# Decoder layer on one core: the work behind the value products done once for two tasks, splits before roots, six leading self pairs

## What is computed

```python
x = _layernorm(x + _L0_attn_ref(x, wq, bq, wk, bk, wv, bv, wo, bo))      # self: softmax(q k^T / sqrt(8)) v, then wo
x = _layernorm(x + _L0_xattn_ref(ctx, x, ctx, Wk, Wq, Wv, Wo))           # cross: 8x8 weights per head, then Wo
x = _layernorm(x + _L0_ffn_ref(x, W1, b1, W2, b2))

def _layernorm(x, eps=1e-05):
    m = mean(x); v = var(x)
    return (x - m) / sqrt(v + eps)

def _qlinear(x, W, b):           # twice in _L0_ffn_ref, with an exact gelu between
    xq, sx, zx = _affine_quantize(x)      # scale from min and max over the whole tensor
    wq, sw = _sym_quantize(W)
    return einsum('bsh,oh->bso', xq - zx, wq) * (sx * sw) + b
```

## Time and profile before

| | us |
|---|---|
| median of 3 runs | 369.61 |
| lowest and highest | 368.77, 369.62 |
| the profiled execution | 368.67 |
| its span, first to last instruction | 366.9 |
| DVE busy | 328.6 (90%) |
| PE busy | 267.3 (73%) |
| ACT busy | 255.5 (70%) |
| POOL busy | 189.1 (52%) |

### The profile page before, as it was taken

One profiled execution on the slowest core, in us unless ns is written; L12 is line 12 of the kernel. 1 busy time (PEld: TensorE's weight loads), 2 busy tenths in 40 slices (PEclk: granted clock), 3 DMA queues, 4 the chain that ended last, 5 costly groups with the idle time before them and its releaser, 6 DMA issues.

```text
span 366.9 us, 13218 instructions
## 1 busy us (share of the span) xinstructions
PE 267.3 (73%) x4899; PEld 170.7 (47%) x4899; DVE 328.6 (90%) x718; ACT 255.5 (70%) x504; POOL 189.1 (52%) x382
## 2 busy tenths in 40 slices
PE   3669878998888988889888898888783466102960
PEld 2446545565655655656565565555452121001540
DVE  5657798899999999999999999999989599998994
ACT  2126877687878878788787888778672499605965
POOL 5244778566665665656666566665222005400385
PEclk9999999899999999999999999999997586755995
DMA  1352332324233233232332324332000000000024
GB/s 50 99 153 67 85 90 61 89 76 113 75 91 104 75 98 96 76 97 82 105 98 70 95 76 118 84 90 79 15 5 1 0 0 0 0 0 3 0 88 143
DMA packets 48998, 25.19 MB, mean 69 GB/s; under 512 B 6440, under 2 KB 48808, under 8 KB 48936
## 3 DMA queue, kind: packets, MB, share of 16 engines
q1 hardware_dynamic: 48216, 24.02, 22.9%
q10 hardware_dynamic: 720, 0.33, 0.3%
HBM read 9.39 MB, written 2.10 MB: 31 GB/s over the span
## 4 chain that ended last, share of the span: by engine, by line
DVE 40%; PE 17%; issue 17%; POOL 12%; SPq 6%; DMA 4%; ACT 3%; DVEq 0%; POOLq 0%; ACTq 0%
DVE neg_max L787 15%; DVE h_ext L893 5%; DVE h_ext L894 5%; PE ps L1019 4%; PE ps L1045 4%; SPq L351 4%; PE ps L1061 3%; POOL rstd L489 2%; DVE arena_q L929 2%; ACT probs L622 2%; DVE r_sum L797 2%; DMA arena_h<-parts_cq 2%; POOL o_root L556 2%; DVE arena_q L804 1%; PE ps L1087 1%
## 5 line engine op out<-in xcount | busy, mean ns | idle before, releaser
L787 DVE TENSOR_REDUCE neg_max<-ps 128x8 f32<-128x1024 f32 x128 | 155.7, 1217 | 13.2 <-PE ps L1019 11.8
L611 ACT ACTIVATE probs<-ps 128x1024 f32<-128x1024 f32 x64 | 65.6, 1024 | 19.8 <-PE ps L1026 18.6
L1019 PE MATMUL ps<-arena_h 31*128 31x128 f16 x1024 | 52.8, 222 | 35.0 <-DVE neg_max L787 22.9
L622 ACT ACTIVATE probs<-ps 128x1024 f32<-128x1024 f32 x64 | 65.6, 1025 | 17.6 <-PE ps L1026 16.1
L1019 PEld LDWEIGHTS ps<-arena_h 31*128 31x128 f16 x1024 | 30.9, 94 | 67.8 <-DVE neg_max L787 40.2
L486 POOL TENSOR_TENSOR var_eps<-mean_var,eps_col 128x1 f32<-128x1 f32 x64 | 12.2, 191 | 81.6 <-DVE mean_var L834 81.6
L1026 PE MATMUL ps<-arena_h 32*128 32x128 f16 x1024 | 51.6, 219 | 0.5 <-ACT probs L611 0.5
L1045 PE MATMUL ps<-probs,arena_q 128*32 128x128 f32 x1024 | 42.2, 284 | 0.9 <-issue 0.9
L1045 PE MATMUL ps<-probs,arena_h 128*32 128x128 f32 x1024 | 41.2, 279 | 0.2 <-ACT probs L611 0.2
L489 POOL TENSOR_TENSOR rstd<-var_eps,minus_half 128x1 f32<-128x1 f32 x64 | 35.2, 550 | 5.2 <-PE ps L1045 0.2
L1026 PEld LDWEIGHTS ps<-arena_h 32*128 32x128 f16 x1024 | 29.5, 93 | 1.5 <-issue 0.9
(11 more groups left out here) (152 smaller groups left out, 641.2 us busy)
## 6 DMA issues: line engine op xcount, KB each, us to landing
arena_h<-parts_sq SPq DMA_DIRECT2D x48, 64.0 KB, 1.9
arena_h<-parts_ck SPq DMA_DIRECT2D x48, 64.0 KB, 2.0
arena_h<-parts_cq SPq DMA_DIRECT2D x48, 64.0 KB, 2.1
arena_h<-parts_sk SPq DMA_DIRECT2D x45, 64.0 KB, 2.0
...
```

Source lines behind the costliest of these rows:

```text
L611: act.activation(probs[1][:, :], ps_s2, ACT.Exp, scale=SCALE).then_inc(ex, 1)
L622: act.activation(probs[0][:, :], ps_s2, ACT.Exp, scale=SCALE).then_inc(ex, 1)
L787: dve.tensor_reduce(neg_max[b.par][:, HH * half:HH * half + HH], ps_s1.rearrange("p (h k) -> p h k", h=HH), AXX, ALU.max, negate=True).the ...
L1019: ins = pe.matmul(ps_s1[:, at:at + S], q[r:r + MAX_AT, j, :], kk[r:r + MAX_AT, j, :], start=True, stop=True, skip_group_check=True)
```

## The change

Pairs take the place of tasks in all that lies behind the value products. `u_sb` is 128x512, `r_sum` 128x32, `att` and `attT` hold both tasks. `whole(k)` gives the task at k only if it is the second of its pair. With `w, x, v = whole(k - 2), whole(k - 3), whole(k - 4)` the reciprocal, `att`, the root and the norm come in odd slots only, and the residual and `bn_stats` in even slots only.

```diff
-LEAD_PAIRS = 5
+LEAD_PAIRS = 6
-QK_AT, V_AT, CK_AT, FILL_AT, VC_AT, BIAS_AT = 5, 4, 5, 4, 3, -1
+Q_AT, K_AT, V_AT, CK_AT, FILL_AT, VC_AT, BIAS_AT = 6, 5, 4, 5, 4, 2, -2
...
+def whole(k):
+    t = task(k)
+    return t if t is not None and t.half == 1 else None
...
             def slot(k):                                            # POOL
-                v = task(k - 4)
+                i = k_pair(k)
+                if i:
+                    pool.wait_ge(eqk, 2 * i + 1)
+                    split(pool, "sq", q_full[:, :], i)
+                i = cq_pair(k)
+                if i is not None:
+                    pool.wait_ge(txe, i + 1)
+                    split(pool, "cq", cq_full[i % RING][:, :], i)
+                v = whole(k - 4)
                 if v is not None:
-                    pool.wait_ge(ag, v.pos + 1)
-                    pool.tensor_tensor(var_eps[v.par][:, :], mean_var[v.par][:, 1:2], eps_col[:, :], ALU.add).then_inc(ve, 1)
+                    pool.wait_ge(ag, 2 * v.at + 2)
+                    pool.tensor_tensor(var_eps[v.lane][:, :], mean_var[v.lane][:, :, 1],
+                                       eps_col[:, 0:1].broadcast_to([128, 2]), ALU.add).then_inc(ve, 1)
...
             def slot(k):                                            # ACT, after the exponential and max_rows
+                if q_pair(k - 1) is not None and q_pair(k - 1) >= LEAD_PAIRS:
+                    q_out(q_pair(k - 1))
+                if v_pair_of(k - 1) is not None:
+                    v_out(v_pair_of(k - 1))
                 if a is not None:
...
-                if z is not None:
-                    act.wait_ge(pv, 2 * z.pos + 2)
-                    need(act, tu, z.pos)
-                    act.copy(u_sb[:, :], ps_u[:, 0:2 * S]).then_inc(ue, 1)
+                if zz is not None:
+                    act.wait_ge(pv, 2 * zz.pos + 2)
+                    need(act, tu, zz.at)
+                    act.copy(u_sb[:, :], ps_u).then_inc(ue, 1)
...
                 maximum(0)                                          # DVE
                 if w is not None:
-                    u = ps_t[:, 0:2 * S].rearrange("p (h c) -> p h c", c=16)
-                    dve.wait_ge(tu, w.pos + 1)
+                    u = ps_t.rearrange("p (h c) -> p h c", c=16)
+                    dve.wait_ge(tu, w.at + 1)
                     dve.reciprocal(r_sum[:, :], u[:, :, E]).then_inc(rs, 1)
                 if v is not None:
-                    dve.wait_ge(rq, v.pos + 1)
...
+                    for i in range(2):
+                        dve.wait_ge(bs, 2 * v.at + i + 1)
+                        dve.bn_aggr(mean_var[v.lane][:, i, :], stats[:, i, :]).then_inc(ag, 1)
...
+                if v is not None:                                   # after maximum(1)
+                    dve.wait_ge(rq, v.at + 1)
+                    for i in range(2):
...
+                        dve.tensor_scalar(dst, src, mean_var[v.lane][:, i, 0:1], rstd[v.lane][:, i:i + 1],
+                                          ALU.subtract, ALU.mult).then_inc(xn, 1)
```

389 lines of the change are left out of this document (211 added, 178 removed).

## The result

The changed kernel takes 396.19 us (median of four runs, 394.50 to 396.65) against 369.19 us for the kernel before (367.32 to 369.62, timed on the same chip). The ratio is 1.0755, 95% interval 1.0721 to 1.0788. The forecast was 375.9 us with a range of 367.5 to 385.0: the sign was right, the size was not, and the time lies outside the range. The profiled execution took 396.65 us with a span of 394.7 us; that of before had a span of 366.9 us.

What follows compares the result with a forecast made beforehand. DVE and PE take turns, a 1.73 us floor per half, with a late root stalling q-split slots. 368.67 + 0.2 start + 3.7 cycles - 2.4 tail + 1.3 + 1.1 + 3.3 clock = 375.9 us; range 367.5 to 385.

Steps and rivals of the forecast that it cites:

- The floor of 1.73 us, and halves without own work at it: Steady slots: the turn through PE between maxima sets at least 1.73 us a half, whatever DVE sheds.
- q out at 2.01, split to 3.45, root 0.70 for two columns, end 4.50: Odd slots with a q split: POOL's root waits behind the split, ending 1.5 us after DVE wants the norm at 3.00.
- Rival 1: Slots with a q split: q out before about 0.5 us, so root not late; 354.6 us; chance 0.12.
- The second norm comes first, the half costs 3.40: Odd slots with a q split: second norm issues before POOL's second split part; half 3.40 instead of 1.73 us.
- rival 5: Stalled slots: second norm also loses to POOL, 0.58 us each, 5.8 more, with more clock drops; 380 to 388; chance 0.17.
- Odd slot, first half 1.86: DVE's maximum, reciprocal, two aggregations and merged att in an odd slot's first half sum to 1.86 us.
- the cover of 1.73 us: PE's work of about 1.6 us a half fits below the 1.73 us turn, so moved projections cost nothing.
- Odd slot, second half 1.73 where nothing stalls: Odd slot's second half: maximum and two norms take 1.55 us without a wait, so the half takes 1.73.
- Cycle 15.77: Steady cycle of four slots, eight halves with one stalled: 15.77 us, 0.37 above before.
- Three clock drops, +3.3: Granted clock falls in three of ten stalled slots, 1.1 us each; +3.3 us, ends 0 and +11.
- Start, +0.2 with bounds -2 and +3: Up to slot 9: shrunken halves against waits such as about 3 us in slot 5; net +0.2 us.
- Tail -2.4 and +1.3, drain +1.1: Slots 49 to 61: shorter pairs -2.4 us, slot 57's stall +1.3; drain: open roots in slots 63 and 65, +1.1.

Runs made afterwards that it cites:

- e13: Changed kernel with ScalarE's copy of q out of PSUM moved ahead of the slot's first exponential, behind the lead only: 377.8 us, ratio 1.026.
- e8: Changed kernel with GpSimd waiting behind the root until both norms are done, before the k split: 382.6 us, ratio 1.037.
- e7: e6 with TensorE's four turns of the value products ahead of the turns of x1 and of the maxima: 372.9 us, ratio 1.012.
- e2: Changed kernel with the q split behind the root for the leading pairs alone: 391.2 us, ratio 1.061.
- e3: Changed kernel with the split keys' first transfers issued behind the first value copy on ScalarE: 395.3 us, ratio 1.074.
- e6: Changed kernel with q split behind the root, first value copy ahead of key transfers, leading q fills behind the next slot's row of maxima: 375.0 us, ratio 1.017.
- e12: e7 plus norms before q split, last cq split behind root, two loads a slot later, clearings in even slots, weight rounding in slots 6 and 8: 375.5 us.

## Right and wrong, step by step

- *The floor of 1.73 us, and halves without own work at it*: right. The undisturbed halves of the even slots are at 1.71 to 1.73.
- *q out at 2.01, split to 3.45, root 0.70 for two columns, end 4.50*: right, 1.95, 3.39, 0.71 and 4.33. But DVE wanted the norm at 3.45 and not at 3.00, since its first half is longer (below), so the wait is 0.91 us and not 1.5. That the late q makes the stall is shown by e13, where nothing but the place of its copy is changed; with the late root the hold-up of the norms went too, so e13 gives the price of both. Rival 1 named the right condition, an early q; its time of 354.6 us was still not reached by that alone, since the lead and the terms below stand against it in e13 as well.
- *The second norm comes first, the half costs 3.40*: the mechanism was wrong and the number right by accident. The second norm lost to POOL's next instruction (rival 5); measured from a later start, 2.23 instead of 1.86, the half still came out at 3.43. Counted from the slot's start the maximum came at 5.66 and not at 5.26. e8 gives the price, 0.78 us a slot; I had 0.58. The rule that the forecast cited from the Trainium skill (SBUF — State Buffer, Who interferes with whom), whoever issues first makes the other block, fits 1.38 us against 0.60: the pair is held up as long as GpSimd works. Which of the two issued first can't be seen in the row of the pair.
- *Odd slot, first half 1.86*: mis-sized, 2.23 with turns of x1 and 1.96 without. I had costed TensorE's work at nothing under the cover of 1.73 us, but the four turns of the value products are not free: the reciprocal waits for them, and they stood behind the turns of x1 (0.44) and of the maxima. With them first (e7) it is 1.91. That is 0.37 + 0.10 us a cycle.
- *Odd slot, second half 1.73 where nothing stalls*: mis-sized, 1.91 in every merged kernel here. The maximum of 119.49 in the changed kernel ended at 120.70, the scores started at 120.96 and the next maximum at 121.40:

```profile
120.96 0.21 PE L1084 MATMUL ps<-arena_h 31*128 31x128 f16 x1 [0.37 <-DVE neg_max L844]
```

  Before the first scores of a new pair TensorE starts 0.26 us after the maximum, not 0.06 as in the earlier trace rows. The earlier trace rows are slot 30, an even slot, in which no pair is opened: I had taken one slot as the pattern of all, and gave the turn of 1.73 us to halves in which it is longer. For its own half the reading of the 1.88 us as DVE's chain was right (there the scores start at 149.33, 0.06 after the maximum, and the next maximum waits for nothing). Here the scores open a pair and have to wait for its stacks too, long landed; that these further waits take the 0.2 us is argued, not shown. It is 0.18 us a cycle in slots without a stall, and it goes for every merged kernel; before, the second halves of odd slots took 1.90 to 2.6 us too, and DVE's own chain of 1.88 covered most of it.
- *Cycle 15.77*: measured 16.44 undisturbed (158.98 to 175.42), above it by 0.37 + 0.03 + 0.10 + 0.18, to rounding. Ten cycles, 6.7 us.
- *Three clock drops, +3.3*: three it was, in slots 26, 34 and 42, a half of 2.72 instead of 1.73 each time. With the shorter first halves behind them and the first cycles the steady slots are 4.4 us above ten undisturbed cycles. That a stall brings drops is borne out: e13 has none in the ten cycles, and e8 none behind a half of 2.65 us. That it was three is luck: seven of the ten stalled slots had none, and the number was two in e2 and four in e3, whose steady slots have the same program. Why one stall is followed by a drop and another isn't stays open.
- *Start, +0.2 with bounds -2 and +3*: this is the step that failed, +9.9. Nearly half of the error of 20 us is here. Without it the time would still have been about 387 us, above the range: the other failed step is the cycle, by the two mis-sized halves above. For the start I had taken "about 3 us" for slot 5, which cost 4.8, and set it against gains that did not come. Not costed at all were: the norms of slots 5 and 7 behind the clearings of 0.35 to 0.95 us each (2.23 and 1.93 us for 0.6), the row of maxima behind the fill in slot 3 (1.76), the first value copy behind three issues (1.0), and two drops of the clock. e2 shows slot 5 at its place, e8 the clearings, e3 the value copy, e6 the row of maxima (together with the value copy). The rounding of the weights ahead of an exponential (e12: 2.1 us in slot 4) is no part of the +9.9, since the kernel before has it in the same slots. Some 1.7 us at least are the scatter of this execution. A bound of +3 for a stage of which only one wait was priced was no bound.
- *Tail -2.4 and +1.3, drain +1.1*: +1.4 and +1.8 measured. The tail has the same mis-sized halves, 2.5 us; slot 57 took its second half in 3.06, as forecast. What the 0.7 us more behind slot 61 are was not looked into, and stays open.

The sum of the misses is 9.7 + 6.7 + 1.1 + 2.5 + 0.7 = 20.7 us, the difference of the profiled execution's 396.65 us to the forecast.
